# One AdaLN-conditioned quantised FFN kernel: x loaded by quadrants and turned on VectorE, w_gate in twelve loads, int16 weight codes, a split last tile

## What is computed

```python
selected_W = W[cat_ids]; selected_b = b[cat_ids]
cond = jnp.einsum('bsd,bdh->bsh', x, selected_W) + selected_b[:, None, :]
h = act_qdq(cond)                       # scale = max|cond| / 32767, over everything
up = act_qdq(h @ lpbq_dequant(w_up).T)
gate = act_qdq(h @ lpbq_dequant(w_gate).T)
sig = fixed_qdq_u16(jax.nn.sigmoid(gate))
gate = act_qdq(gate * sig)
o = act_qdq(gate * up)
out = x + o @ lpbq_dequant(w_down).T
```

## Time and profile before

| | |
|---|---|
| median of three runs | 958.22 us |
| the profiled execution | 959.29 us, of which the span from first to last instruction is 957.5 us |
| PE busy / PEld busy | 893.6 us (93%) / 477.3 us (50%) |
| VectorE busy / ACT busy | 658.0 us (69%) / 420.9 us (44%) |
| mean granted TensorE clock | 0.97 of full speed |
| HBM read / written | 173.94 MB / 73.66 MB, 259 GB/s over the span |

### The profile page before, as it was taken

How to read it: one execution, slowest core, us unless ns; L and a number is a source line. 1 busy time by engine, 2 the same in 40 slices (tenths; PEclk the granted TensorE clock), 3 DMA queues, 4 the chain that set the end, 5 groups by cost and what they waited for, 6 DMA issues and landing times. The chain is left out here.

```text
span 957.5 us, 13114 instructions
## 1 busy us (share of the span) xinstructions
PE 893.6 (93%) x4736; PEld 477.3 (50%) x4736; DVE 658.0 (69%) x792; ACT 420.9 (44%) x454; POOL 3.1 (0%) x12
## 2 busy tenths in 40 slices
PE   8999999999999999999999999990079999999998
PEld 7999994444444444444444444440034444444443
DVE  2349869655667454379899889669998887755511
ACT  1112326323223223299798882229865544444000
POOL 0000000000000000000000000000000000000000
PEclk9999999999999999999999999995579999999999
DMA  8999872453574343499999735999977999987221
GB/s 320 401 397 328 321 258 100 149 165 137 163 242 131 136 142 128 172 347 421 400 398 390 262 124 208 404 421 414 418 274 293 328 342 341 337 289 281 88 88 66
DMA packets 81587, 254.32 MB, mean 266 GB/s; under 512 B 32082, under 2 KB 32082, under 8 KB 77714
## 3 DMA queue, kind: packets, MB, share of 16 engines
q1 hardware_dynamic: 46354, 198.72, 55.3%
q10 hardware_dynamic: 35200, 55.20, 16.4%
HBM read 173.94 MB, written 73.66 MB: 259 GB/s over the span
## 5 line engine op out<-in xcount | busy, mean ns | idle before, releaser
L609 ACT ACTIVATE stage<-bank 128x512 f32<-128x512 f32 x186 | 108.6, 594 | 212.8 <-PE bank L861 162.9
L1137 DVE TENSOR_REDUCE tile_max<-stage 128x1 f32<-128x1536 f32 (+1 forms) x62 | 108.4, 1749 | 34.6 <-ACT stage L609 31.7
L859 PE MATMUL bank<-xq_head,wt_gate 128*128 (+1 forms) x336 | 127.4, 379 | 0.3 <-DVE xq_head L1124 0.3
L859 PE MATMUL bank<-xq_head,wt_up 128*128 x336 | 127.4, 379 | 0.1
L860 PE MATMUL bank<-xq_head,wt_up 128*128 x336 | 127.3, 379 | 0.0
L861 PE MATMUL bank<-xq_head,wt_up 128*128 x336 | 127.3, 379 | 0.0
L861 PE MATMUL bank<-xq_head,wt_gate 128*128 (+1 forms) x336 | 127.3, 379 | 0.0
L860 PE MATMUL bank<-xq_head,wt_gate 128*128 (+1 forms) x336 | 127.3, 379 | 0.0
L773 PE MATMUL bank<-xt,w_ring 128*128 128x128 f32 x960 | 112.1, 275 | 0.0
L773 PEld LDWEIGHTS bank<-xt,w_ring 128*128 128x128 f32 x960 | 109.9, 192 | 0.0
L1017 DVE SCALAR_TENSOR_TENSOR wparts<-wf,scal,wparts 128x512 f16<-128x512 f32 (+2 forms) x36 | 27.0, 749 | 62.8 <-ACT wparts L552 62.8
(11 more groups left out here) (205 smaller groups left out, 1368.7 us busy)
## 6 DMA issues: line engine op xcount, KB each, us to landing
up_ring<-up_scratch SPq DMA_DIRECT2D x54, 768.0 KB, 7.2
w_ring<-in_L_cond_W_dram SPq DMA_DIRECT2D x30, 1024.0 KB, 7.3
gate_scratch<-stage ACTq DMA_DIRECT2D x32, 768.0 KB, 3.4
gate_ring<-gate_scratch SPq DMA_DIRECT2D x32, 768.0 KB, 8.6
up_scratch<-stage ACTq DMA_DIRECT2D x30, 768.0 KB, 7.8
product_scratch<-prod_ring SPq DMA_DIRECT2D x19, 768.0 KB, 9.7
back_ring<-product_scratch SPq DMA_DIRECT2D x19, 768.0 KB, 13.0
gate_even<-gate_scratch SPq DMA_DIRECT2D x16, 768.0 KB, 8.4
```

What stands on the lines that cost most here:

```text
L609: nc.scalar.activation(stage[:, q % 2, n % PIECE_TILES, :], up_bank(i, n), ACT.Copy)\
L859: nc.tensor.matmul(bank, w_hi, x_hi, start=(k == 0), stop=False)
L1137: V.tensor_reduce(tile_max[:, side, bass.ds(Q * i + q, 1)], stage[:, q % 2, :, :].rearrange("p t c -> p (t c)"), AX.X, ALU.max, apply_abso ...
```

## The change

- **x.** load_x_batch is gone. A batch's x now comes in four transfers (QUADS): quadrant q takes features 128q to 128q + 127 of all 128 tokens into partitions 32q to 32q + 31, as four runs of 512 bytes for each partition. SP issues those of the first four batches (load_first_x), ACT those of every later one (load_x in ACT's program), behind its bias addition for the batch four before.
- **Turning x.** VectorE transposes in blocks of 32 x 32 (V.transpose, 128 x 512 in one instruction) from x_ring to xt, which has four slots (XT); it runs three batches ahead. PE's transposes and ACT's copies are gone.
- **Bias.** ACT adds it, in four activations of 128 x 128 for each batch, for chunks 0 to 6; VectorE keeps the last chunk. VectorE's maximum of a chunk comes one batch later than before.
- **w_gate** comes in 12 transfers of 256 KB, one behind each matrix of batches 5 to 16; quantising starts at batch 17 (QUANT_AT), ACT's high_part follows at 18.
- **quantise_slice** has two passes in place of three, for all three weights: the first writes int16 codes (wq), the conversion rounds.
- **Start.** The bias product and four spare products come ahead of the first batch; half_bank names other banks for batch 1.
- **Tail.** The last tile is multiplied as two halves of 256 columns into two banks (last_quarter), and finished and stored in halves; the x of the last two tiles is loaded ahead into x_tail, their results go to y_tail.

The diff, cut to its core:

```diff
-                if not first:
-                    turned = held(sp, b - BPC + 1)
-                    sp.wait_ge(x_turned, turned)
-                sp.dma_start(x_ring[:, r, :], x_flat[bass.ds(b, 1), :, :]...).then_inc(x_in[r], 16)
+            def load_first_x(r):
+                for q in range(QUADS):
+                    sp.dma_start(x_ring[32 * q:32 * q + 32, r, :, :],
+                                 x_flat[r, :, q * P:(q + 1) * P].rearrange("(t p) j -> p t j", p=32)).then_inc(x_in[r], 16)
...
             for r in range(BPC):
-                    load_x_batch(i, r, False)
                     load_w_batch(i, r, False)
-                    if r in gate_parts:
-                        at = SLICES * gate_parts[r]
-                        sp.dma_start(wf[:, at:at + SLICES, :], wg_view[:, at:at + SLICES, :]).then_inc(wgate_in, 16)
+                    if isinstance(i, int) and 0 <= BPC * i + r - GATE_AT < WSLICES:
+                        n = BPC * i + r - GATE_AT
+                        sp.dma_start(wf[:, n, :], wg_view[:, n, :]).then_inc(wgate_in[n // SLICES], 16)
...
-            def copy_xt(i, r, first):          # ACT
...
+            def add_bias(i, r):                # ACT
+                act.wait_ge(cond_done, b + 1)
+                for m in range(KH):
+                    src = (half_bank(r, m) if halved else psum[r])[:, m * S:(m + 1) * S]
+                    done = nc.scalar.activation(cond_head[...], src, ACT.Identity, bias=bias[...])
+                done.then_inc(cond_copied, 1)
+            def load_x(i, r):                  # ACT
+                act.wait_ge(x_turned, held(act, b + 1))
+                for q in range(QUADS):
+                    act.dma_start(x_ring[32 * q:32 * q + 32, r, :, :],
+                                  x_flat[bass.ds(b + BPC, 1), :, q * P:(q + 1) * P]...).then_inc(x_in[r], 16)
...
-                for k in range(KH):            # PE, turn_x
-                    mm = nc.tensor.transpose(psum[4 + r % 2][:, k * S:(k + 1) * S], by_part[:, k, :], ident32[:, :])
...
+            def turn_x(i, r, ahead):           # VectorE
+                dve.wait_ge(x_in[slot], 16 * QUADS * (j + 1))
+                if not (isinstance(i, int) and BPC * i + r + ahead < XT):
+                    dve.wait_ge(cond_done, BPC * i + r + ahead - XT + 1)
+                V.transpose(xt[:, slot, :, :].rearrange("p k (t s) -> p k t s", s=32),
+                            x_ring[:, slot, :, :].rearrange("p t (j k) -> p k t j", k=KH)).then_inc(x_turned, 1)
...
-                V.tensor_tensor(by_block, by_block, blocks(wrecip, w, n), ALU.mult).then_inc(w_scaled, 1)
-                V.tensor_scalar(flat, flat, ROUND, ROUND, ALU.add, ALU.subtract).then_inc(w_rounded, 1)
-                V.tensor_tensor(by_block, by_block, blocks(wstep, w, n), ALU.mult).then_inc(w_stepped, 1)
+                V.tensor_tensor(codes, by_block, blocks(wrecip, w, n), ALU.mult).then_inc(w_rounded, 1)
+                V.tensor_tensor(by_block, codes, blocks(wstep, w, n), ALU.mult).then_inc(w_stepped, 1)
...
+                for half, bank in enumerate((down_bank(1, BPC - 1), down_bank(0, 0))):   # PE, last_quarter
+                    cols = slice(half * H // 2, (half + 1) * H // 2)
...
+            for half, bank in enumerate((down_bank(1, BPC - 1), down_bank(0, 0))):       # VectorE
+                dve.wait_ge(right_done if half else left_done, 1)
+                V.scalar_tensor_tensor(out=y_tail[:, 1, cols], in0=bank[:, cols], scalar=k_y, in1=x_tail[:, 1, cols], ...)
```

More of the change, by code:

```diff
@@ L39 @@
 HALVED = 2
+QUADS = 4
+WARM_BEFORE, WARM_AFTER = 9, 4
+XT = 4
+GATE_AT = 5
+STEPS_AT = 16
+QUANT_AT = 17
 LOCAL = 4
@@ L96, in adaln_ffn @@
         w_ring = place("w_ring", 96 * K, [BPC, KH, H], f32)
-        x_ring = place("x_ring", 128 * K, [BPC, H], f32)
-        xt = place("xt", 136 * K, [2, KH, S], f32)
+        x_ring = place("x_ring", 128 * K, [BPC, QUADS, P], f32)
+        xt = place("xt", 136 * K, [XT, KH, S], f32)
         R = 144 * K
@@ L125, in adaln_ffn @@
         y_out = place("y_out", R + 40 * K, [2, H], f32)
+        x_tail = place("x_tail", R + 30 * K, [2, H], f32)
+        y_tail = place("y_tail", R, [2, H], f32)
         C = R + 56 * K
@@ L498, in finish_chunk @@
             def finish_chunk(i, pairs_left, last):
-                for r in range(BPC):
+                for r in range(BPC // 2 if last else BPC):
                     if r < pairs_left:
@@ L510, in finish_chunk @@
                                  y_out[:, r % 2, :]).then_inc(y_out_done[r % 2], 16)
-                    if not last or r < 2:
+                    if not last:
                         load_x(BPC * i + r + 2, r)
@@ L748, in _, with cond_matmul @@
             pe.wait_ge(spare_made, 1)
-            spare_matmuls(8)
-            pe.wait_ge(ident_made, 1)
-            def turn_x(i, r, first):
+            spare_matmuls(WARM_BEFORE)
+            def cond_matmul(i, r, first, last=False):
                 b = BPC * i + r
-                pe.wait_ge(x_in[r], 16 * i + 16)
-                if not first or r >= 2:
-                    pe.wait_ge(x_copied, b - 1)
-                by_part = x_ring[:, r, :].rearrange("s (p k) -> s k p", k=KH)
-                for k in range(KH):
-                    mm = nc.tensor.transpose(psum[4 + r % 2][:, k * S:(k + 1) * S], by_part[:, k, :], ident32[:, :])
-                mm.then_inc(x_turned, 1)
-            def cond_matmul(i, r, first, last=False, between=None):
-                b = BPC * i + r
-                pe.wait_ge(x_copied, b + 1)
+                pe.wait_ge(x_turned, b + 1)
                 pe.wait_ge(w_in[r], 16 * i + 16)
@@ L941, in _ @@
                         down_quarter(2 * pair + h, h, q, False)
+            for q in range(Q):
+                down_quarter(CHUNKS - 2, 0, q, False)
+            for q in range(Q):
+                last_quarter(q)
         @block.vector
@@ L1076, in _, with cond_step @@
-            cond_chunk(4, 2)
-            with dve.Fori(5, CHUNKS - 1) as i:
-                cond_chunk(i, 0)
+            def cond_step(i, r):
+                b = BPC * i + r
+                fixed = isinstance(i, int)
+                if not fixed or b + XT - 1 < B:
+                    turn_x(i, r, XT - 1)
+                if not fixed or QUANT_AT <= b < QUANT_AT + WSLICES:
+                    quantise_slice(0, b - QUANT_AT)
+                if not fixed or b >= QUANT_AT + 2:
+                    low_part(0, b - QUANT_AT - 2, b - QUANT_AT - 2)
+                if r == 1 and not (fixed and i == 0):
+                    chunk_max(i - 1)
+                if fixed and b < STEPS_AT + 2:
+                    for m in range(KH):
+                        if b == (GATE_AT + SLICES * m + SLICES if m < KH - 1 else STEPS_AT):
+                            gate_blocks(m)
+                    if b == STEPS_AT:
+                        dve.wait_ge(wblocks_maxed, KH)
+                        weight_steps(0, WG)
+                    if b == STEPS_AT + 1:
+                        weight_scale(0, WG)
@@ L1101, in _ @@
                                 bias[:, B - 1, ks].unsqueeze(2).to_broadcast([P, KH // 2, S]),
-                                ALU.add).then_inc(cond_copied if half else last_half_copied, 1)
+                                ALU.add).then_inc(last_copied if half else last_half_copied, 1)
                 if half == 0:
```

263 lines of the change are left out of this document (135 added, 128 removed).

## The result

The changed kernel takes 982.4 us (median of four runs, 980.5 to 987.2) against 958.2 us for the kernel before (957.95 to 959.72) beside it: ratio 1.026, 95% interval 1.022 to 1.030. The forecast was 946.3 us, so its sign is wrong too, and the time lies far outside the range. The profiled execution took 982.26 us, its span is 980.4 (957.5 before).

A forecast was written before the change was run, and what follows sets the result against it. PE was taken to set the pace, with the DMA engines close behind. Terms of -13.8 + 0.3 + 2.0 + 0.4 - 0.8 = -11.9 us gave 946.3 us against the median of 958.22; range 944.0 to 956.5.

The forecast's parts named there:

- PE's 13.8 us: Conditioning stage: without PE's transposes, 31 batches at 3.62 us take 112.2 us instead of 126.0, saving 13.8 us.
- rival 4: Conditioning stage: products do not close up, spacing stays near 4.05 us because f32 weights or x are late; 957.7, chance 0.04.
- the start: Kernel start: more x issues ahead of the first matrix make batch 0 end at 14.3 or 14.4, +0.3 us.
- w_gate: Conditioning stage: w_gate's packets behind 12 matrices put DMA in arrears beyond the ring's lead, a stall of +2.0 us (0 to 5).
- ACT: Conditioning stage: activations, issues and high_part total 3.5 us a batch, under 3.62; +0.4 us (0 to 5) allowed.
- The DMA term: Conditioning stage: DMA work per batch is 2.54 us of matrix plus 0.95 of x, 3.49, under PE's 3.62.
- rival 2: Conditioning stage: small packets are slow outright; beyond 46 ns each the kernel is slower, 973 at 60 ns; chance 0.12.
- rival 1: Conditioning stage: narrow x transfers are slow, 37 to 43 ns a packet, DMA sets the pace; 952, chance 0.24.
- The landing time: Conditioning stage: x lands perhaps 4 us after its issue, leaving about 3.4 us to spare before it is needed.
- VectorE: Conditioning stage: with a 0.7 us transpose, VectorE needs 3.4 us a batch in batches 17 to 28, against 3.62.
- rival 3: Batches with high_part: ACT or VectorE becomes the bound, transpose at 1.1 making VectorE 3.8; 950, chance 0.10.
- The tail: Kernel end: x loaded ahead, last finish and store in halves, 256-column products at unchanged time; -0.8 us.

## Why the prediction was wrong, step by step

**PE's 13.8 us: right in kind, a little small.** The spacing closed up where PE was fed, rival 4 is out, and without x traffic the kernel takes 946.1 us, to 0.2 the forecast. That closeness is in part luck, since errors cancel in it. The spacing is 3.58 and not 3.62, so from batch 2's start to the gate product the run without x takes 110.8 us where it was 125.4, 14.5 less; against that, batch 2 starts 2.3 us later than before (20.43 against 18.18), where the start had +0.3; and the 2.4 us allowed for w_gate and ACT were not needed.

**The DMA term: the step that failed.** I made a batch 2.54 us of matrix and 0.95 of x, 3.49, under PE's 3.62 "by a hair". By the table's row of the change it was 2.94 and 1.17, 4.1. The price of x's packet was nearly right (30 ns forecast; 27.4 measured alone, 34.5 to 35.1 beside matrices); that the matrices' packets stay at their price (318 ns forecast and measured before, 362 now), which the sum took for granted, was wrong. Counted against x alone, (4.1 - 2.54) x 16 / 512 is 49 ns a packet, past the 46 at which rival 2 said the change loses. So rival 2's outcome came by rival 1's cause, which I had capped at 43 ns because I asked only what a narrow transfer costs itself, not what it does to its neighbours. (Its count was off too: with four transfers of 512 byte runs a batch has 384 more data packets and 48 more of 4 bytes, not 48 "of every kind".) With a margin of 0.13 us a batch the forecast also had no right to 0.50.

31 batches at 4.1 and 9 us for w_gate, less 5.3 of lead, are 131 us; the stage took 144 from batch 0's end (16.1) to batch 31's (160.1). **The landing time** is the second failed step, and beside wide transfers the larger one (21 us by the square above). I had x land "perhaps 4 us" after its issue and 3.4 to spare. It landed after 11.9 in 20:60 and 5.4 in 100:140. From one batch's end to the start of the fourth behind it go 1.1 of bias additions, 1.3 of issues (0.32 each on a free queue), 11.9 and 1.1 of transpose: 15.4 us where three batches at 3.62 have 10.9. With the 5.4 of 100:140 the sum is 8.9 and fits, so the loop as added up here holds the first part of the stage and not the last. Asking two batches earlier gave 7 us back, GpSimd's lead 3. How the other 6 to 10 divide between this loop and low clock stands open; 960 product instructions at 282 in place of 275 ns are 6.7 us, part of them in the shadow of the DMA engines.

**VectorE**: 1.10 us for the transpose, not 0.7, so 3.63 a batch and not 3.4; rival 3's condition (1.1) held, though not the 3.8 a batch that it drew from it, and its mechanism is what is left in the run with one wide transfer, 951.8 against its 950. **ACT**: four activations took 1.14 us in a row, 1.1 forecast; but where its queue was full three issues took 5.15 us (at 61.39) in place of 1.3, a cost that the sum did not have. **The start**: eight issues took 4.03 us, the matrix went out at 6.16 in place of 5.3, and batch 0 ended at 16.1 in place of 14.3: 1.8 us missed. **w_gate**: without x traffic PE had no wait at all, so the 2.0 us forecast for it was too much there; with quadrants it is not separable. **The tail**: forecast 0.8. The last product starts 2.99 us ahead of the end (980.4 less 977.41) where it was 3.93, which is 0.94, and the 256 column products stand 0.11 us apart, so their weight loads cost nothing:

```profile
977.30 0.27 PE L948 MATMUL bank<-wt_down,o_odd_tail 128*128 128x256 f16 x1
...
977.41 0.27 PE L949 MATMUL bank<-wt_down,o_odd_tail 128*128 128x256 f16 x1
```

## What to carry to other kernels

A transfer's price is not its own packets' time: before changing the shape of a small stream beside a large one, ask what the large one's packets will take, and where the DMA engines stand within a few per cent of the bound, put the change down as a coin toss at best. Keep loads over all partitions, and don't give them a small outermost dimension: with 4 only 0.27 of the engines' time was used. If a layout needs quadrants, load it where the DMA engines are idle; asking for it earlier gave back only 3 to 7 of the 24 us. Read a pace from start to start, since a row's busy time can be longer. And when an engine takes over work in order to free the bound, set its sum against the new pace and not the old: VectorE at 3.63 against 3.58 carries every delay to the end.

## What the runs showed of the hardware that was not expected

- Four transfers of 64 KB into 32 partitions each cost 27.4 ns a 512 byte packet alone, as much as into 128 partitions (27.6); beside 8 KB packets 34.5 against 27.5, and those packets' own time rose from 40 to 42 engine-us for a MB beside wide transfers to 45 to 55 beside narrow ones. Why is not shown. In each comparison the narrow form also has an outermost dimension of 32 where the wide one has 128, and no run separates how a transfer is shared out over the engines from the partitions that it reaches. The rule on ports that rival 1 cites from the Trainium skill, SBUF — State Buffer, "Door 1: The DMA port swizzle", is not settled either: alone, the narrow form moved 4.46 MB in 80 us, 56 GB/s, far below the 218 GB/s that one estimates from that section's figures for partitions 0 to 31 (8 ports at 27.2 GB/s).
- On one queue the narrow form was worst: 281 to 317 GB/s at a share of 1.06 to 1.07, against 405 (1.02) in 20:60 for the wide 2 KB form.
- An issue takes 0.32 us on a free queue and up to 5.15 us for three on a full one, and the engine's next compute instruction waits behind it.
- A VectorE block transpose of 128 x 512 f32, read with a stride of four, takes 1.10 us against 0.69 for an element-wise pass of that size.
- GpSimd issued four transfers in some 2.2 to 2.4 us, and the 512 byte runs of its transfers appear as packets of 4096 bytes.
